# Layer 2: rows fetched by an index table instead of scattered, and the normalisation begun in the attention

## What is computed

```python
x = x + s * g                                   # end of layer 1
xn = _layernorm(x, axis=-1)
s = _L1_attn_ref(xn)                            # for each position, softmax attention over the 8 entries and features
g = _silu(_L1_ffn_ref(xn, gate_w, w1, w2, w3))  # 8 experts, each row goes to its best two
x = x + s * g

def _L1_ffn_ref(x, gate_w, w1, w2, w3):         # xt: 2048 rows of 512
    probs = jax.nn.softmax(xt @ gate_w.T, axis=-1)
    top_vals, top_idx = jax.lax.top_k(probs, 2)
    top_vals = top_vals / jnp.sum(top_vals, axis=-1, keepdims=True)
    h1, h3 = jnp.einsum('th,efh->tef', xt, w1), jnp.einsum('th,efh->tef', xt, w3)
    expert_out = jnp.einsum('tef,ehf->teh', _silu(h1) * h3, w2)
    y = jnp.einsum('te,teh->th', w_full, expert_out)
```

## Time and profile before

| what | us |
|---|---|
| median of three runs (1498.78 to 1500.48) | 1499.13 |
| the profiled execution | 1501.16 |
| its span, first to last instruction | 1499.2 |
| `attention`, 167 to 760.8 | 594 |
| `across_batch`, 760.8 to 875.5 | 115 |
| `experts`, 875.5 to 1446 | 570 |
| `combine`, 1446 to the end | 53 |

### The profile page before, as it was taken

How to read it: one execution, slowest core, us unless ns; L and a number is a source line. 1 busy time by engine, 2 the same in 40 slices (tenths; PEclk the granted TensorE clock), 3 DMA queues, 4 the chain that set the end, 5 groups by cost and what they waited for, 6 DMA issues and landing times. The chain is left out here.

```text
span 1499.2 us, 24968 instructions
## 1 busy us (share of the span) xinstructions
PE 1349.1 (90%) x7870; PEld 1149.3 (77%) x7871; DVE 699.4 (47%) x1617; ACT 565.9 (38%) x1775; POOL 615.0 (41%) x516
## 2 busy tenths in 40 slices
PE   6989899999999999999877579999999999999940
PEld 6934487878787878888547469999999999999930
DVE  6352376666676766666447332223222222232237
ACT  3421276655556656666534221212212111122124
POOL 0020155444444545454325445172662617451135
PEclk9889999999999999999878689999999999999985
DMA  8035720000000000000015566273772728555247
GB/s 290 1 84 143 277 93 15 15 14 14 14 14 14 14 25 17 14 14 15 7 58 177 195 225 187 99 247 109 238 243 96 268 72 289 171 169 182 72 126 258
DMA packets 67068, 171.47 MB, mean 114 GB/s; under 512 B 6448, under 2 KB 15040, under 8 KB 66704
## 3 DMA queue, kind: packets, MB, share of 16 engines
q0 software_dynamic: 25776, 98.73, 19.9%
q1 hardware_dynamic: 35632, 61.95, 12.9%
q10 hardware_dynamic: 5616, 10.23, 1.9%
HBM read 125.26 MB, written 45.61 MB: 114 GB/s over the span
## 5 line engine op out<-in xcount | busy, mean ns | idle before, releaser
L1681 PE MATMUL bank<-expert_weights,rows_t 128*128 x1872 | 359.4, 347 | 1.8 <-DVE rows_t L1613 1.6
L1681 PEld LDWEIGHTS bank<-expert_weights,rows_t 128*128 128x128 f32 x1872 | 340.8, 189 | 5.8 <-issue 2.6
L958 ACT ACTIVATE room<-bank,room 128x256 f32<-128x256 f32 (+1 forms) x512 | 208.9, 415 | 114.0 <-DVE room L891 113.9
L986 POOL TENSOR_TENSOR room<-room 128x1024 f32<-128x1024 f32 (+1 forms) x128 | 187.9, 1468 | 120.1 <-DVE room L868 120.1
L742 PE MATMUL bank<-room 96*128 (+2 forms) x1024 | 189.1, 327 | 0.0
L1625 DVE TENSOR_TENSOR x_keep<-x_keep,bank 128x400 f32<-128x400 f32 x78 | 44.5, 571 | 304.2 <-ACT x_keep L1568 302.9
L1093 POOL TENSOR_TENSOR expert_weights<-x_keep,expert_weights 128x1600 fp32r<-128x1600 f32 (+2 forms) x49 | 160.2, 3270 | 54.9 <-DMA expert_weights<-w 54.6
L742 PEld LDWEIGHTS bank<-room 96*128 96x128 f32 x1024 | 159.1, 191 | 13.7 <-issue 0.4
L1704 PE MATMUL bank<-expert_weights,act_t 128*128 x702 | 165.6, 389 | 1.0 <-ACT act_t L1573 1.0
L993 POOL TENSOR_TENSOR room<-room 128x256 f32<-128x256 f32 x128 | 93.2, 728 | 173.5 <-DVE room L932 172.2
L1704 PEld LDWEIGHTS bank<-expert_weights,act_t 128*128 128x128 f32 x702 | 131.5, 188 | 25.6 <-issue 1.3
(11 more groups left out here) (231 smaller groups left out, 1773.4 us busy)
## 6 DMA issues: line engine op xcount, KB each, us to landing
x_keep<-w POOLq DMA_DIRECT2D x28, 800.0 KB, 5.0
expert_weights<-w POOLq DMA_DIRECT2D x28, 800.0 KB, 6.5
x_keep<-w POOLq DMA_DIRECT2D x14, 768.0 KB, 6.0
expert_weights<-w POOLq DMA_DIRECT2D x14, 768.0 KB, 7.7
rows_by_expert<-room SPq DMA_DIRECT2D x1, 9984.0 KB, 29.0
x_keep<-rows_by_expert SPq DMA_DIRECT2D x39, 256.0 KB, 4.0
results_by_row<-x_keep ACTq DMA_DIRECT2D x39, 256.0 KB, 4.6
room<-wo SPq DMA_DIRECT2D x16, 512.0 KB, 5.8
```

Of the source, the lines that this page charges most:

```text
L958: last = sc.activation(Pr[:, m % 4, hh, 0:w], scores_bank(m)[:, w * hh:w * hh + w], ACT.Exp, bias=nb[:, par, hh:hh + 1], accum_out=sm[:, p ...
L986: g.tensor_tensor(pr, pr, rs[:, one[1] % 2].unsqueeze(2).broadcast_to([P, 4, w]), ALU.mult).then_inc(normed, 1)
L1681: last = mm(psum(2 * hf + w)[:, 0:HF], xgT[:, par, of_x, P * k:P * k + P], W[:, ds(off + (of_w * SLOT + (k * 2 + w) * FF + hf * HF), HF)], ...
```

## The change

Four parts. (1) In `attention`, `early_rows` normalises tiles 0 to 13 in the last entry's steps: the epsilon at m = 6, POOL's power in the same step, the refinement at m = 7, two tiles in each of m = 8 to 14. The zero fill of `s.xs` goes. The semaphores of the first stage are given back and used again, so POOL clears them one by one at the head of `attention`. (2) In `across_batch`, SP stores all 16 normalised tiles to DRAM (`s.xn`), between the third and the fourth weight chunk. The high parts of chunks 0 to 2 come by three transfers that POOL issues; ACT copies those of chunks 3 to 6, chunk 3 ahead of the softmax's exponential and 4 to 6 ahead of its rounds. POOL subtracts chunks 0 to 3, and 5 and 6 when the slots are there; DVE subtracts chunk 4. The logits are turned by 16 transposes, and two reductions add the four parts. (3) The 32 scattering transfers go. Instead DVE and PE make `s.index`: for each of the 39 blocks and each of its 128 places the row that stands there. DVE forms comparisons (`find_blocks`, `name_tiles`, `find_places`) in rounds 0 to 4, ACT scales one in round 1, PE adds 32 matmuls in its iteration 5, and DVE writes the index in round 5, with the block tables that stood at the end. POOL then gathers blocks 0 and 1 straight to the experts' row places. (4) In `experts`, POOL gathers blocks 2 to 5 into two staging places and stores them to `s.xs`; in each of the first 17 iterations of its weight loop it gathers two more blocks and stores them. SP loads a block when its store has landed, ACT waits for the first two stores, and POOL's two subtractions at the stage's start are gone.

```diff
+def gather_rows(s, b, to, landed):
+    s.nc.gpsimd.indirect_dma_start(
+        out=to, out_offset=None, in_=s.xn,
+        in_offset=bass.IndirectOffsetOnAxis(ap=s.index[:, b:b + 1], axis=0)).then_inc(landed, 16)
+
+def keep_blocks(s, b, rows):
+    n = rows.shape[1]
+    s.nc.gpsimd.dma_start(s.xs[P * b:P * b + P * n, :].rearrange("(t p) n -> p t n", p=P), rows).then_inc(s.rows_there, 16)
...
@@ attention
+    def early_rows(dve, m):
+        v = nc.vector
+        if m == 6:
+            dve.wait_ge(stats_done, EARLY_ROWS * 3)
+            v.tensor_scalar(s.mv[:, 0:EARLY_ROWS, 1], s.mv[:, 0:EARLY_ROWS, 1], LN_EPS, None,
+                            ALU.add).then_inc(early_var, 1)
+        if m == 7:
+            dve.wait_ge(early_seed, 1)
+            root_refined(v, Chain(dve, early_dve), early_rs, early_root, s.mv[:, 0:EARLY_ROWS, 1])
+        if m >= 8 and 2 * (m - 8) < EARLY_ROWS:
+            if m == 8:
+                dve.wait_ge(s.x1_stored, 16 * EARLY_ROWS)
+            for t in (2 * (m - 8), 2 * (m - 8) + 1):
+                v.tensor_scalar(X[:, t], X[:, t], s.mv[:, t, 0:1], early_rs[:, t:t + 1], ALU.subtract,
+                                ALU.mult).then_inc(s.xn_ready, 1)
...
+        if last_entry(b) and b == LAST and m == 6:
+            pool.wait_ge(seed_ready, 1)
+            pool.wait_ge(early_var, 1)
+            g.tensor_tensor(early_rs, s.mv[:, 0:EARLY_ROWS, 1], early_root, ALU.pow).then_inc(early_seed, 1)
...
-            nc.gpsimd.memset(zeros, 0.0).then_inc(s.zeros_ready, 1)
+            for of_first_stage in s.done_with:
+                pool.sem_clear(of_first_stage)
+            nc.gpsimd.memset(early_root, -0.5).then_inc(seed_ready, 1)
...
-            sp.wait_ge(s.zeros_ready, 1)
-            sp.dma_start(s.xs.rearrange("(n p) h -> p n h", p=P),
-                         zeros.unsqueeze(1).broadcast_to([P, NBLK, D])).then_inc(s.blank, 16)
@@ across_batch, SP
+            for c in range(3):
+                bring_chunk(sp, s, 0, c, raw[:, c % 3]).then_inc(s.raw0_in[c % 3], 16)
+            for t in range(NT):
+                keep_rows(t)
+            for c in range(3, NCH):
+                sp.wait_ge(pool_low, c - 2)
+                bring_chunk(sp, s, 0, c, raw[:, c % 3]).then_inc(s.raw0_in[c % 3], 16)
@@ across_batch, POOL
+            for c in DMA_HIGH:
+                at, rows, n = CHUNKS[c]
+                bring_chunk(pool, s, 0, c, s.W[:, at:at + n]).then_inc(high0_in[c], 16)
...
             for c in POOL_LOW:
-                pool.wait_ge(first_high, c + 1)
+                if c in DMA_HIGH:
+                    pool.wait_ge(high0_in[c], 16)
+                else:
+                    pool.wait_ge(first_high, c - len(DMA_HIGH) + 1)
+                pool.wait_ge(s.raw0_in[c % 3], 16 * (c // 3 + 1))
                 low_of(s, c, raw_of(c), 0).then_inc(pool_low, 1)
-            pool.wait_ge(s.blank, 16)
             pool.wait_ge(slots_ready, 1)
-            for t in range(NT):
-                for k in range(2):
-                    nc.gpsimd.indirect_dma_start(
-                        out=xs, out_offset=bass.IndirectOffsetOnAxis(ap=s.slots[:, t, k:k + 1], axis=0),
-                        in_=X[:, t], in_offset=None).then_inc(sorted_, 16)
-            pool.wait_ge(sorted_, 16 * 2 * NT)
+            for c in (5, 6):
+                pool.wait_ge(first_high, c - len(DMA_HIGH) + 1)
+                low_of(s, c, raw_of(c), 0).then_inc(pool_low, 1)
+            pool.wait_ge(index_steps, 7)
+            for b in range(2):
+                gather_rows(s, b, s.xg[:, b], s.first_in[b])
@@ across_batch, ACT
-            high_of(0)
+            high_of(3)
             act.wait_ge(p_ex, 1)
             sc.activation(p, p, ACT.Exp).then_inc(p_exd, 1)
-            high_of(1)
+            high_of(4)
+            high_of(5)
+            high_of(6)
@@ across_batch, DVE
+            def find_places(i):
+                at = slice(8 * i, 8 * i + 8)
+                v.tensor_tensor(place_hit[:, at], const("row_ids").unsqueeze(1).broadcast_to([P, 8, P]),
+                                in_block[:, at].unsqueeze(2).broadcast_to([P, 8, P]),
+                                ALU.is_equal).then_inc(index_steps, 1)
...
+                if r == 0:
+                    find_blocks()
+                if r == 1:
+                    name_tiles()
+                if 1 <= r < 5:
+                    find_places(r - 1)
+                if r == 5:
+                    write_index()
+                    block_tables()
@@ experts, POOL
-            pool.wait_ge(first_w2, NCH - KT_PER_D - 1)
+            for b in range(2, 6):
+                gather_rows(s, b, (passing if b < 4 else y)[:, b % 2], s.rows_got)
             for stored in s.messages_stored:
                 pool.wait_ge(stored, 16)
             bring_high(0)
+            pool.wait_ge(s.rows_got, 16 * 4)
+            keep_blocks(s, 2, passing)
+            keep_blocks(s, 4, y)
             for j in range((E - 1) * NCH):
                 e, c = 1 + j // NCH, j % NCH
                 more = j + 1 < (E - 1) * NCH
+                blocks = range(6 + 2 * j, min(8 + 2 * j, NBLK))
                 if more:
                     bring_raw(j + 1)
                 if more and c + 1 < NCH:
                     bring_high(j + 1)
                 pool.wait_ge(raw_in[j % 2], 16 * (j // 2 + 1))
                 pool.wait_ge(high_in[j % 2], 16 * (j // 2 + 1))
+                if blocks:
+                    pool.wait_ge(s.rows_there, 16 * (2 + j))
+                    for b in blocks:
+                        gather_rows(s, b, passing[:, b % 2], s.rows_got)
                 at, rows, n = CHUNKS[c]
                 low_of(s, c, stage[0:rows, j % 2, 0:n], e % 2 * 2 * SLOT).then_inc(s.converted, 1)
+                if blocks:
+                    pool.wait_ge(s.rows_got, 16 * (blocks[-1] - 1))
+                    keep_blocks(s, blocks[0], passing[:, 0:len(blocks)])
                 if more and c + 1 == NCH:
                     bring_high(j + 1)
@@ experts, SP
+            for b in range(2, NBLK):
+                sp.wait_ge(s.rows_there, 16 * max(2, b // 2))
+                sp.wait_ge(x_turned, b - 1)
+                load(b, b % 2)
```

More of the change, by code:

```diff
@@ L38 @@
 PT_RING = 8
+EARLY_ROWS = NT - 2
 XN_BUFS, GATE_BUFS = 4, 3
@@ L146, in build @@
         s.x1_stored, s.converted, s.kept_in = (s.sem(n) for n in ("x1_stored", "converted", "kept_in"))
-        s.raw0_in = [s.sem(f"raw0_in{i}") for i in range(2)]
+        s.xn_ready = s.sem("rows_normal")
+        s.raw0_in = [s.sem(f"raw0_in{i}") for i in range(3)]
         s.messages_stored = [s.sem(f"messages_stored{i}") for i in range(4)]
@@ L162, in build @@
                 s.XNT = sb(inner, "xn_turned", [P, NT, KT_PER_D, P])
-                first_stage(s)
+                with ExitStack() as held:
+                    s.semaphores = held
+                    first_stage(s)
+                s.semaphores, s.done_with = ctx, s.taken
             s.qs = sb(scope, "q_latent_parts", [P, 2, 2, P], F32R)
@@ L208, in sem @@
     def sem(self, name):
-        return self.ctx.enter_context(self.nc.semaphore(name))
+        taken = self.semaphores.enter_context(self.nc.semaphore(name))
+        if self.semaphores is not self.ctx:
+            self.taken.append(taken)
+        return taken
     def carve(self, *shape, dt=F32):
@@ L1264, in _ @@
             dve.wait_ge(lt, 1)
-            step.then(v.tensor_copy(p, psum(7)[:, 0:P].rearrange("p (t e) -> p t e", t=NT)))
+            for hf in range(2):
+                quarters = s.bank[2 + hf][:, :].rearrange("p (t k e) -> p t e k", t=NT // 2, k=4)[:, :, 0:E]
+                last = v.tensor_reduce(p[:, NT // 2 * hf:NT // 2 * hf + NT // 2], quarters, AX.X, ALU.add)
+                step(last)
+            step.wait()
             step.then(v.tensor_reduce(top, p, AX.X, ALU.max))
@@ L1303, in _, with find_blocks @@
             v.tensor_copy(s.slots, slotf).then_inc(slots_ready, 1)
+            def find_blocks():
+                dve.wait_ge(xn_stored, 16 * NT)
+                dve.wait_ge(batched_p, POOL_XP)
+                dve.wait_ge(batched_v, NT - POOL_XP)
+                flat = slotf.rearrange("p t k -> p (t k)")
+                step.then(v.tensor_scalar(in_block_int, s.slots.rearrange("p t k -> p (t k)"), P - 1, None,
+                                          ALU.bitwise_and))
+                step.then(v.tensor_copy(in_block, in_block_int))
+                step.then(v.tensor_tensor(block_at, flat, in_block, ALU.subtract))
+                v.tensor_tensor(block_hit, const("block_rows").unsqueeze(1).broadcast_to([P, 2 * NT, NBLK]),
+                                block_at.unsqueeze(2).broadcast_to([P, 2 * NT, NBLK]),
+                                ALU.is_equal).then_inc(index_steps, 1)
@@ new lines, in write_index, with block_tables @@
+            def write_index():
+                dve.wait_ge(indexed, 1)
+                found = psum(7)[:, 0:2 * NBLK].rearrange("p (w b) -> p w b", w=2)
```

(43 more changed lines are left out.)

135 lines of the change are left out of this document (69 added, 66 removed).

## The result

The changed kernel takes 1536.72 us (median of 4 runs, 1535.04 to 1541.08), the kernel before 1499.38 on the same chip: a ratio of 1.025, 95% interval 1.0238 to 1.0263, 37 us slower. The forecast was slower, 1517, with 1541 as the upper end. The direction and the mechanism hold; the size is about half of what came. The profiled execution takes 1537.57, its span is 1535.5.

What follows compares the result with a forecast made beforehand. Bound by PE in the experts, with POOL's weight loop barely ahead, and by scatters in `across_batch`. Stalls 30.0 plus restarts 7.2 less gains 19.1 give +18.1: 1517 us median, forecast's range 1500 to 1533, with rivals 1484 to 1541.

Steps and rivals of the forecast that it cites:

- Attention, +2.5: In `attention`: early normalisation that doesn't all fit costs 2.0 us, POOL's semaphore clears 0.5.
- Head, 0: Head of layer 2: no gain, since chunk 3's landing keeps Exp at about 790; bounds 8 us earlier, 5 later.
- Rounds, -17.7: In `across_batch`: without scatters, slots to last table take 54.9 us instead of 72.7; bounds 48 and 72.7.
- the hand-over, -3.9: Start of `experts`: blocks 0 and 1 already lie in place, so PE turns at once, 3.9 us saved.
- rival B: Rounds' unnamed waits aren't the scatters' and stay, or go with heavy DMA traffic: 1541 us at most; chance 0.13 with another rival.
- The period, P = 9.97: POOL's weight loop in `experts`: an iteration with a pair of gathers takes L + 6.27 = 9.97 us, L being the store's landing.
- the 3.7 that I took: POOL's loop in `experts`: L, issue to landing of a 512 KB store, 3.7 us, between 2.75 and 4.8.
- Stalls, 30.0: In `experts`: PE waits for late weights of experts 1, 2 and 3 by 6.2, 13.8 and 10.0 us, sum 30.0.
- the prediction's own formulas: Stalls ahead of experts 1, 2 and 3 from POOL's period P: 6P - 53.6, 6P - 46.0 and 2P - 9.9 us.
- Restarts at a lower clock: In `experts`: after each of three stalls PE restarts at a lower clock, 2.4 us each, 7.2 in all.
- outer end (1541): Whole kernel: upper end of the range, 1517 plus the 24 us lost in the rounds, should their unnamed waits come back.
- rival A: POOL's loop in `experts`: stores land in about 2.1 us, P = 8.4, time 1496, 1488 with the quicker head; chance 0.29.

Runs made afterwards that it cites:

- run 7: Changed kernel with 2 instead of 14 tiles normalised early in the attention, the other 14 at the head of layer 2: 1533.69 us.
- run 2: Changed kernel with ACT's high copy of chunk 3 moved behind Exp: 1528.94 us.
- run 1: Kernel before the change with its 32 scattering transfers left out, so the experts multiply zeros: 1472.15 us, ratio 0.9807.
- run 11: Kernel before the change with 32 gathers from DRAM in the place of its 32 scatters, same places and bytes: 1492.35 us, ratio 0.9945.
- run 8: Changed kernel whose stores of a pair of blocks write a quarter of the columns, 128 KB in place of 512: 1525.12 us.
- run 9: Changed kernel whose POOL loop issues an iteration's gathers ahead of the next chunk's two weight transfers instead of behind them: 1554.38 us.
- run 4: Changed kernel with blocks 2 to 5 gathered and stored at the end of `across_batch`, where POOL is idle, instead of at the experts' start: 1531.16 us.
- run 3: Changed kernel with the same gathers and stores spread over other chunks of POOL's list and its waits for a place of weights: 1491.83 us, ratio 0.9934.

## Why the prediction was right in its direction and short in its size

**Attention, +2.5.** Right in sign, too high: POOL's first instruction of layer 2 comes 593.4 us after PE's first of the attention, 592.8 before, and run 7 prices the early rows at 1.3.

**Head, 0.** Nearly: +2.8 from the start of layer 2 to the slots, Exp at 791.4 against a forecast of 790, and run 2 shows that chunk 3 is what holds it.

**Rounds, -17.7, and the hand-over, -3.9.** Right: -17.4 and -3.2, and round by round too: 8.0, 7.5, 5.6, 5.6, 5.6, 8.4 and 4.5 for the first seven, forecast 7.5, 7.7, 5.0, 5.8, 5.8, 8.1 and 5.0. That the scatters are the cause, which the prediction took with a doubt (rival B), is shown by run 1; what about them it is, run 11 tells only in part.

**The period, P = 9.97.** Mis-sized: 10.7. This is the step that failed first. The landing was not the error: 3.2 us, below the 3.7 that I took. The estimate from the Trainium skill (DMA: Bandwidth & Descriptors, Anatomy of one DMA) was 3.2, and the trace agrees; for 128 KB the same fit gives an estimate of 2.3, where run 8 has 2.2. Two other terms were booked at 0.1 or at nothing. From the landing to the first gather pass 0.8 us (916.69 + 3.2 is 919.9, the gather begins at 920.67), the same in all iterations of experts 1 and 2 in which the store ends the wait. In run 9, where a gather waits for the store alone and not for two weight transfers too, it is 0.27; why the one is longer isn't shown. The store's own issue, 0.76 to 0.78 us on POOL, lies inside the landing. And gathered rows were said to land during the subtraction; they do so only in some iterations, the mean wait over the twelve stores of experts 1 and 2 that follow a large chunk is 0.6, the longest 1.7; a part of this may be the 1.6 MB of weights ahead of them in POOL's queue (not shown, see run 9). Gathers cost 2.34 instead of 2.52. So 3.2 + 0.8 + 2.34 + 3.65 + 0.6 = 10.6, near the 10.7 of the trace.

**Stalls, 30.0.** With 10.7 the prediction's own formulas give 10.6, 18.2 and 11.5, together 40.3; measured are 8.3, 17.6 and 15.2, 41.0, and 1.6 later. Expert 2 is thus explained by the period. Expert 1 looks so by luck, as two misses offset each other there: its weights are whole 85.8 us after PE's first turn (945.6), where the formula has 81.9 with a period of 10.7, because the opening of POOL's list takes longer (its first gathers in the loop begin 17.1 after PE's first turn, forecast 13.7); and PE arrives 78.0 after its first turn instead of 71.3. Expert 3 needed more:

```profile
1083.76 3.66 POOL L1148 TENSOR_TENSOR expert_weights<-x_keep,expert_weights 128x1600 fp32r<-128x1600 f32 x1
...
1091.54 3.67 POOL L1148 TENSOR_TENSOR expert_weights<-x_keep,expert_weights 128x1600 fp32r<-128x1600 f32 x1
...
1097.80 3.41 POOL L1148 TENSOR_TENSOR expert_weights<-x_keep,expert_weights 128x1536 fp32r<-128x1536 f32 x1 [0.74 <-DMA expert_weights<-w]
...
1105.42 3.42 POOL L1148 TENSOR_TENSOR expert_weights<-x_keep,expert_weights 128x1536 fp32r<-128x1536 f32 x1 [2.81 <-DMA expert_weights<-w]
...
1109.72 1.28 POOL L1148 TENSOR_TENSOR expert_weights<-x_keep,expert_weights 32x512 fp32r<-32x512 f32 x1
```

Its last four chunks, which carry no gathers, come 7.8, 6.3, 7.6 and 4.3 apart where I took 4.93. In the first of these POOL still waits 2.0 for the last gathered rows, in the next two 0.7 and 2.8 for weights. The weight loads land in 8.0 us in the median here, 6.5 in the earlier trace rows; that they come back to the old pace only slowly behind the gathers is argued, not shown.

**What wasn't in the sum:** block 2's rows, 3.5 us late behind its store, though run 4 shows that they cost nothing so long as expert 1's weights are later still. Restarts at a lower clock: 8.7 (L1825 367.4 us busy in place of 359.4, transposes 0.7) against 7.2.

`experts` by its parts: 42.6 + 3.5 + 8.7 = 54.8 of 55.7, forecast 37.2. Where the missing 18.5 lie is told by PE's first matmuls for experts 1, 2 and 3: up to the first PE takes 15.0 us longer than before (forecast 6.2), to the second 19.4 (16.2 with a restart), to the third 17.7 (12.4), and behind it 3.7 (2.4). Up to expert 1, the largest miss, POOL's chain alone counts: expert 1's weights are whole 85.8 us after PE's first turn and not 77.5, the formula's value at P = 9.97; of these 8.3 us 4.4 are six longer periods and 3.9 the opening. Over all three experts the period is worth 10.3 by the formulas, more than half of what is missing. The measured time lies above the forecast's own range (1533) and below its outer end (1541), which had been put there for another case. Two slips in the working changed nothing: by its own terms rival A breaks even at P = 8.78, L = 2.51, not 8.68 and 2.41, and 72.7 less 54.9 is 17.8.

## What to carry to other kernels

Work that is added to an engine which feeds another is priced by its period times the deadlines it meets: write the loop out as that engine lists it, with every issue instruction and every wait, and put the additions where the feeding has slack (1492 us against 1537 for the same transfers, run 3). Turning the order round on one queue can just move the wait: the store that run 9 put behind 1.6 MB of weights landed in 5.0 us instead of 3.2. And of two lateness terms that meet at one point only the later one counts, in a saving as in a loss.

## What was not expected of the hardware

A POOL store of 512 KB lands in 3.2 us where a POOL load of that size took 4.8; behind 1.6 MB of its queue the same store takes 5.0 in the median (run 9). From a store's landing to POOL's next gather pass 0.8 us in the changed kernel and 0.27 in run 9. And 32 indirect transfers in a row lengthen a stage of other engines, whether they write (72.7 us from slots to last table) or read (65.0), against 47.0 without.
